# In the experts stage, TensorE transposes the next tile's rows before, not after, it transposes this tile's inner values

## The reference

```python
probs = jax.nn.softmax(logits / TEMP, axis=-1)
w, idx = jax.lax.top_k(probs, K)                      # K = 2 of E = 8
h = jax.nn.silu(jnp.einsum('btd,edf->betf', xn, W1))  # D = 256 to H = 1024
y = jnp.einsum('betf,efd->betd', h, W2)               # back to D = 256
out = jnp.einsum('bte,betd->btd', wdense, y)
return out + res
```

## Time and profile before

| what | value |
|---|---|
| median of 3 runs | 4235.97 us (4231.28 to 4237.2) |
| the profiled execution, its own time | 4207.76 us |
| its span, first to last instruction | 4205.6 us |
| TensorE busy | 3397.4 us, 81% |
| VectorE busy | 2157.8 us, 51% |
| ScalarE busy | 1951.0 us, 46% |
| POOL busy | 936.5 us, 22% |

### The profile page before, as it was taken

How to read it: one execution, slowest core, us unless ns; L and a number is a source line. 1 busy time by engine, 2 the same in 40 slices (tenths; PEclk the granted TensorE clock), 3 DMA queues, 4 the chain that set the end, 5 groups by cost and what they waited for, 6 DMA issues and landing times. The chain is left out here.

```text
span 4205.6 us, 82054 instructions
## 1 busy us (share of the span) xinstructions
PE 3397.4 (81%) x25752; PEld 2498.6 (59%) x25753; DVE 2157.8 (51%) x6691; ACT 1951.0 (46%) x4754; POOL 936.5 (22%) x724
## 2 busy tenths in 40 slices
PE   6888888858699588888988869999996419999990
PEld 3555555557688366666666657777775306666660
DVE  4776777768677355556555534555554301111116
ACT  4777777823322366555665535656663101111110
POOL 0000000034100566667666400000000350000005
PEclk9999999977799799999999989999998559999995
DMA  2000000010200222212222110000001621000004
GB/s 73 12 13 12 12 12 14 7 47 20 93 1 1 84 61 58 52 49 60 57 59 50 41 48 17 21 21 16 16 17 56 208 84 30 30 30 29 29 29 120
DMA packets 120194, 177.79 MB, mean 42 GB/s; under 512 B 23776, under 2 KB 75424, under 8 KB 119328
## 3 DMA queue, kind: packets, MB, share of 16 engines
q1 hardware_dynamic: 113696, 156.61, 12.7%
q0 software_dynamic: 6144, 16.79, 1.3%
HBM read 90.88 MB, written 32.11 MB: 29 GB/s over the span
## 5 line engine op out<-in xcount | busy, mean ns | idle before, releaser
L893 ACT ACTIVATE a_t<-a_t,a_neg 128x512 f32<-128x512 f32 (+3 forms) x1024 | 642.5, 633 | 8.6 <-DVE a_neg L1070 7.2
L720 PE MATMUL a_T<-ident,a_t 128*128 128x128 f32 x3328 | 506.1, 287 | 106.2 <-ACT a_pT L884 56.0
L884 ACT ACTIVATE a_pT<-a_T 128x512 f32<-128x512 f32 (+3 forms) x896 | 416.5, 501 | 321.9 <-PE a_T L720 320.2
L720 PEld LDWEIGHTS a_T<-ident,a_t 128*128 128x128 f32 x3328 | 383.1, 145 | 300.9 <-issue 281.0
L1065 DVE CUSTOM_DVE_ANT_0 a_t<-a_A,a_table 128x384 f32<-128x384 f32 (+3 forms) x512 | 225.5, 487 | 316.4 <-PE a_A L697 311.2
L1065 DVE CUSTOM_DVE_ANT_0 a_t<-a_A,a_decay 128x512 f32<-128x512 f32 x512 | 322.9, 687 | 96.9 <-PE a_A L685 96.9
L2076 PE MATMUL experts_H<-ex_w,experts_xgT 128*128 x576 | 268.3, 609 | 47.8 <-ACT experts_xgT L2103 47.8
L2126 DVE COPY experts_y<-experts_Y 128x256 f32<-128x256 f32 x72 | 30.5, 424 | 514.2 <-PE experts_Y L2064 514.2
L921 POOL TENSOR_TENSOR a_rsin<-a_rawswapped,a_sin 128x512 f32<-128x512 f32 x128 | 166.8, 1303 | 556.8 <-DMA a_rawswapped<-a_raw 534.5
L2064 PE MATMUL experts_Y<-ex_w,experts_hT 128*128 x1152 | 260.5, 379 | 1.0 <-DVE experts_hT L2135 1.0
L2064 PEld LDWEIGHTS experts_Y<-ex_w,experts_hT 128*128 128x128 f32 x1152 | 218.8, 190 | 61.3 <-issue 35.2
(11 more groups left out here) (278 smaller groups left out, 7043.6 us busy)
## 6 DMA issues: line engine op xcount, KB each, us to landing
a_rawswapped<-a_raw SPq DMA_DIRECT2D x512, 64.0 KB, 2.0
a_invrep<-a_inv_dram SPq DMA_DIRECT2D x64, 256.0 KB, 4.0
ex_w<-in_f_w_dram SPq DMA_DIRECT2D x16, 1024.0 KB, 13.5
moe_sent<-route_zeros SPq DMA_DIRECT2D x1, 9216.0 KB, 29.8
experts_xg<-moe_sent SPq DMA_DIRECT2D x72, 128.0 KB, 2.1
moe_results<-experts_y SPq DMA_DIRECT2D x72, 128.0 KB, 1.7
a_xin<-x_all SPq DMA_DIRECT2D x16, 512.0 KB, 3.5
x_xin<-x_all SPq DMA_DIRECT2D x16, 512.0 KB, 3.4
```

The lines of the kernel that those rows point to most:

```text
L720: mm = pe.transpose(bank[:, kt, :], t_of(u, j, kt * P, (kt + 1) * P), sh.ident[:])
L884: nc.scalar.activation(to, of, ACT.Copy).then_inc(t_empty, 1)
L893: nc.scalar.activation(t_of(u_e % U, j, 0, n), t_of(u_e % U, j, 0, n), ACT.Exp, bias=neg[:, slot, j:j + 1], scale=SCALE, accum_out=total[: ...
```

## The change

In `step` of `experts`' TensorE block the call of `transpose_rows` for the next tile moves from behind the two groups of transposes of `h` to ahead of them. No other line changes; the number of instructions is the same on every engine, and the orders of VectorE, ScalarE, POOL and SyncE are the same rows.

```diff
@@ -2079,15 +2079,15 @@
                 if not first:
                     down(i - 1, 1 - parity)
+                if more:
+
+                    transpose_rows(1 - parity, pair + (parity + 1))
                 for half in range(2):
                     pe.wait_ge(h_act, i * 2 + (half + 1 + 2))
                     for j in range(FT // 2):
                         f = half * (FT // 2) + j
                         mm = pe.transpose(HT[half][:, j, :], h[:, f * P:(f + 1) * P], sh.ident[:])
                     mm.then_inc(ht_full, 1)
-                if more:
-
-                    transpose_rows(1 - parity, pair + (parity + 1))
```

## The result

| | before | after |
|---|---|---|
| median of 5 runs | 4235.97 us (4231.28 to 4239.54) | 4170.31 us (4168.07 to 4172.02) |
| ratio, 95% interval | | 0.9845 (0.9831 to 0.9859) |
| profiled execution, own time | 4207.76 us | 4171.41 us |
| its span | 4205.6 us | 4169.6 us |
| first load of H to last product of `down` | 643.9 us | 582.5 us |

What follows compares the result with a forecast made beforehand. TensorE bounds the experts stage, waiting in every tile for ScalarE's copy before H. 60.9 us from steps 1 to 70 plus 0.5 from step 0 gave 61.4 us off the median 4235.97: 4174.6 us, range 4164 to 4189.

Steps and rivals of the forecast that it cites:

- What bounds the stage: Experts stage: TensorE is the bound; its only repeated wait is H's for ScalarE's copy of transposed rows, 47.8 us.
- The steady step: Steps 1 to 70: H's first load comes 0.87 us earlier per tile, 60.9 us in all.
- the idle row: Rival, PE's idle time before H: only the visible idle goes, about 47 us, 4189 us; chance 6%.
- The remaining 0.06 us: Before H in each steady step: the copy chain stays later than the array's other work, leaving a 0.06 us wait.
- The rule of the Trainium skill: H's first load: pulled ahead, it would lose nothing; rival of 0.93 us a step, 65 us, 4171 us; chance 3%.
- Tile 0: Step 0: H's first load comes at about 3461.7 instead of 3462.21, 0.5 us gained, bounds 0 to 0.95.
- The queues that were passed: VectorE's copies of HT about 0.3 us later, ScalarE's copy 0.87 earlier, SyncE's loads keep their place: cost 0.
- The sum: Whole kernel: 60.9 + 0.5 = 61.4 us gained, taken off the median to give 4174.6 us.
- The offset of 28 us: Whole kernel: runs are 28 us longer than the profiled execution, unexplained; the gain is taken off the median as is.
- The slower rival: Wait for rows ahead of HT: loads over 7.3 us make it slower; at 8 us, 50 us, 4286 us; chance 2%.

Runs made afterwards that it cites:

- again: The changed kernel measured once more beside the kernel before on the same chip: 4169.88 us against 4228.16, ratio 0.9854.
- before_again: The kernel before, unchanged, profiled once more: span 4215.1 us, 643.9 us from H's first load to the last product of `down`.
- late_after: The changed kernel with the loads of rows one tile later: 4563.85 us, ratio 1.0783.
- late_before: The kernel before with the loads of rows one tile later: 4539.76 us, ratio 1.0717.

## Why the prediction was right

*What bounds the stage.* Right: the one repeated wait of TensorE was worth what was lost there, and no other took its place.

*The steady step.* Right: 0.87 us foretold, 8.909 - 8.035 = 0.87 measured over the loop, and half of it with half of the transposes. Taking the distance of two starts rather than the idle time of PE was what made the term right; the idle row would have given 47 us.

*The remaining 0.06 us.* Right: the chain is still the later one. H's first load comes at 3701.89, 0.06 us behind its slot (3700.85 + 9 x 0.109 = 3701.83), and a longer copy costs its full 0.28 us. The rule of the Trainium skill that a 64-deep window pulls weight loads ahead of matmuls ("TensorE: Matmul & The Clock Gate", Part 2) was weighed against this; the trace says that it doesn't reach past a wait at which the sequencer itself stands, since H's load is issued at 3701.89, behind L2073.

*Tile 0.* Foretold 0.5 us, measured 0.4 (8.03 to 7.65 us from its H to the next). The same step is 7.20 us in `again` and 8.20 in `before_again`, so that this term is anything from 0.4 to 1.0, and that the sum comes out to the tenth is in part luck.

*The queues that were passed.* Right for VectorE, ScalarE and SyncE: no wait of `down` but that of the last tile, and loads of rows as quick as before. (The prediction has HT 0.22 us later and VectorE's copies 0.3; with over 2 us of cover it makes no difference.)

*The sum.* 60.9 + 0.5 = 61.4 us, against 643.9 - 582.5 = 61.4 in the stage. The medians differ by 65.7 us, whose interval holds 61.4; in the second comparison they differ by 58. The prediction also wanted the stages before and the length behind the experts stage unchanged; in these two profiles they were 7.0 and 18.4 us longer, in code that is the same in both.

*The offset of 28 us* between the profiled execution and the median, which I had to leave unexplained: most likely 18 of them are `combine`, which was short in that execution, as on one chip of three here; on that chip the kernel before has a median of 4210 us, on the other two 4228 and 4239. This is argued and not shown, and the rest stays open. Leaving it out of the sum was right.

*The slower rival.* Loads as slow as it asks for never came. With loads made late by hand the new order does lose more than the old, by 0.3 us a tile and not 0.87, and through the sequencer and the clock rather than through a held HT; what late loads cost in either order was under-reckoned in the expectations, for want of the clock.

## What to carry to other kernels

In a pipeline written out by hand, the work whose result crosses to another engine and comes back goes first, and the work that nobody is in a hurry for goes behind it; the gain is the work put behind it, counted from start to start, until the chain fits. Ask next where the sequencer stands, not only the array: a wait in front of a register read makes everything behind it late by the read, and reading first cures that. And test a wait that has gone from the list by lengthening what it waited for: if the full price shows, it had no room.

## What the runs showed of the hardware that was not expected

- A wait of a weight load for a DMA holds TensorE's sequencer: the read of a register from SBUF behind it (0.30 us, and 0.9 to 1.1 us up to the first load that depends on it) starts only when the DMA has landed, though the array still has work. With the read and its two waits put ahead of that wait the step fell from 8.10 to 7.98 us.
- Two copies of 0.38 us in a row on ScalarE, 128x256 from PSUM to SBUF, cost 0.28 us more than one.
- The granted clock fell to the 1.2 GHz level behind idle stretches of the array of 3.3 us in nearly every step (`late_after`, 69 of 71) and of 2.5 us in most (`late_before`, 61 of 71), and H then ran at half speed for some 3 us: 3.5 us of wait in each step made it 5.6 us longer (8.04 to 13.64).
